# Both queries-and-keys units ahead of both v units in steps 0 and 2, and a new table of PSUM banks

## The reference

```python
def _attention(xq, xkv, wq, wk, wv, wo, bo):
    q = (xq @ wq).reshape(B, S, N_HEADS, D_HEAD)
    k = (xkv @ wk).reshape(B, T, N_HEADS, D_HEAD)
    v = (xkv @ wv).reshape(B, T, N_HEADS, D_HEAD)
    attn = jax.nn.softmax(jnp.einsum('bihd,bjhd->bhij', q, k) * D_HEAD ** (-0.5), axis=-1)
    return jnp.einsum('bhij,bjhd->bihd', attn, v).reshape(B, S, D_ATTN) @ wo + bo
h = _layernorm(x, ln1_g, ln1_b)
x = _attention(h, h, sa_wq, sa_wk, sa_wv, sa_wo, sa_bo) + x
h = _layernorm(x, ln2_g, ln2_b)
x = _attention(h, cond_emb, ca_wq, ca_wk, ca_wv, ca_wo, ca_bo) + x
h = _layernorm(x, ln3_g, ln3_b)
a, gate = jnp.split(h @ ff_w1 + ff_b1, 2, axis=-1)
return a * jax.nn.gelu(gate, approximate=False) @ ff_w2 + ff_b2 + x
```

## Time and profile before

| | us |
|---|---|
| median of 3 runs | 2865.21 |
| lowest, highest | 2864.95, 2866.52 |
| the profiled execution, device time | 2866.01 |
| its span, first to last instruction | 2864.2 |
| TensorE busy in the span | 2842.0 |
| VectorE, ScalarE, GpSimd busy | 2256.3, 1912.3, 1471.1 |

### The profile page before, as it was taken

The page is one execution under the profiler, slowest core; times in us unless marked ns, Lnnn a source line. Parts: engine busy times, 40 slices in busy tenths (PEclk is TensorE's granted clock), DMA queues, the critical chain, the costliest instruction groups (busy, mean ns, idle before and its releaser), DMA issues.

```text
span 2864.2 us, 72446 instructions
## 1 busy us (share of the span) xinstructions
PE 2842.0 (99%) x25278; PEld 2485.3 (87%) x25278; DVE 2256.3 (79%) x3495; ACT 1912.3 (67%) x6041; POOL 1471.1 (51%) x1310
## 2 busy tenths in 40 slices
PE   8999999999999999999999999999999999999999
PEld 6888888888888888888888888888888889999999
DVE  6888888888888888888888888888888865555554
ACT  6677766677766776777777777777777754444443
POOL 5444444444444444765555555555555544554554
PEclk9999999999999999999999999999999999999999
DMA  5666666666666666667777776666766632222222
GB/s 147 158 162 157 156 157 159 158 154 145 151 151 154 150 148 149 161 166 177 177 172 169 173 171 169 168 164 165 168 168 163 151 100 88 73 73 84 81 73 63
DMA packets 355360, 413.32 MB, mean 144 GB/s; under 512 B 122048, under 2 KB 209472, under 8 KB 355264
## 3 DMA queue, kind: packets, MB, share of 16 engines
q1 hardware_dynamic: 345120, 395.29, 57.4%
q10 hardware_dynamic: 10144, 16.78, 1.6%
HBM read 94.52 MB, written 49.02 MB: 50 GB/s over the span
## 4 chain that ended last, share of the span: by engine, by line
PE 98%; DVE 1%; ACT 1%; POOL 0%; issue 0%; DMA 0%; DVEq 0%; POOLq 0%; ACTq 0%
PE unit_ps L593 54%; PE o_ps L618 17%; PE s_ps L606 14%; PE s_ps L593 12%; DVE neg_max L1021 0%; ACT probs L851 0%; DVE blocks L1035 0%; POOL probs L1253 0%; DMA x_ln<-in_x_dram 0%; ACT qk_hi L882 0%; DVE qk_lo L1046 0%; DVE hT L1016 0%; DVE hT_lo L1059 0%; ACT x_n L828 0%; ACT L828 0%
## 5 line engine op out<-in xcount | busy, mean ns | idle before, releaser
L1253 POOL TENSOR_TENSOR probs<-probs,row_inv 128x1024 f32<-128x1024 f32 x512 | 967.8, 1896 | 893.9 <-DVE row_inv L1026 893.9
L851 ACT ACTIVATE probs<-s_ps,neg_max 128x256 f32<-128x256 f32 x2048 | 950.4, 487 | 403.9 <-DVE neg_max L1021 403.4
L1021 DVE TENSOR_REDUCE neg_max<-s_ps 128x4 f32<-128x1024 f32 x512 | 616.8, 1205 | 62.8 <-PE s_ps L606 58.4
L1035 DVE STREAM_TRANSPOSE blocks<-probs 128x1024 f32<-128x1024 f32 x512 | 633.2, 1237 | 19.9 <-POOL probs L1253 19.9
L593 PE MATMUL unit_ps<-hT_hi,w_hi 128*128 128x256 f32 x2048 | 571.3, 282 | 3.0 <-DVE hT_lo L1059 2.6
L593 PE MATMUL unit_ps<-hT_hi,w_lo 128*128 128x256 f32 x2048 | 554.0, 277 | 0.0
L618 PE MATMUL o_ps<-pT,v_f 128*64 128x256 f32 x4096 | 498.5, 385 | 1.7 <-DVE a_lo L1041 1.7
L593 PE MATMUL unit_ps<-hT_lo,w_hi 128*128 128x256 f32 x1792 | 496.1, 277 | 0.0
L851 ACT ACTIVATION_READ_ACCUMULATOR probs<-s_ps,neg_max 128x1 f32 x2048 | 444.6, 217 | 0.0
L593 PE MATMUL unit_ps<-w_hi,a_hi 128*128 128x256 f32 x1536 | 430.8, 280 | 3.8 <-DVE a_lo L1041 2.8
L593 PE MATMUL unit_ps<-w_lo,a_hi 128*128 128x256 f32 x1536 | 425.7, 277 | 0.0
(11 more groups left out here) (73 smaller groups left out, 6017.8 us busy)
## 6 DMA issues: line engine op xcount, KB each, us to landing
pT<-blocks SPq DMA_DIRECT2D x1024, 256.0 KB, 4.5
rows_t_dram<-row_blocks SPq DMA_DIRECT2D x91, 256.0 KB, 4.4
rows_in<-rows_t_dram SPq DMA_DIRECT2D x91, 256.0 KB, 4.1
x_res<-in_x_dram SPq DMA_DIRECT2D x32, 256.0 KB, 4.1
x_sa_dram<-x_out SPq DMA_DIRECT2D x32, 256.0 KB, 4.3
x_ln<-x_sa_dram ACTq DMA_DIRECT2D x32, 256.0 KB, 4.9
ctx_in<-in_ctx_dram SPq DMA_DIRECT2D x32, 256.0 KB, 4.4
x_res<-x_sa_dram SPq DMA_DIRECT2D x32, 256.0 KB, 4.1
```

What stands on the lines that cost most here:

```text
L851: op = nc.scalar.activation(probs[:, m % 2, r, :].rearrange("p (j b c) -> p j b c", j=IT, c=BLK), scored.rearrange("p (j c b) -> p j b c", ...
L1021: nc.vector.tensor_reduce(neg_max[:, m % RING, :], s_ps[:, m % 2, :, :].rearrange("p h (i j) -> p (h i) j", j=S), AX_X, ALU.max, negate=Tr ...
L1035: nc.vector.transpose(blocks[:, n % 2, :, m % 2, :].rearrange("p b (j r c) -> p r j b c", j=IT, c=BLK), probs[:, m % 2, :, :].rearrange("p ...
L1253: nc.gpsimd.tensor_tensor(probs[:, m % 2, :, :], probs[:, m % 2, :, :], row_inv[:, m % RING, :].unsqueeze(2).broadcast_to([P, ROWS, S]), A ...
```

## The change

In steps 0 and 2 of STEP_UNITS both qk units are put ahead of both v units; in step 2 the x unit moves behind the two qk units. BANK_OF gets a new table. The order lists of the other engines are not edited, but two of them read STEP_UNITS: evacuated_early now picks both qk units in steps 0 and 2, and bank_free finds other last users.

```diff
 STEP_UNITS = (
-    ((("v", 0, 0), "cur"), (("qk", 2), "cur"), (("qk", 3), "cur"), (("v", 0, 1), "cur")),
+    ((("qk", 2), "cur"), (("qk", 3), "cur"), (("v", 0, 0), "cur"), (("v", 0, 1), "cur")),
     ((("qk", 4), "cur"), (("qk", 5), "cur"), (("wo", 0), "prv")),
-    ((("v", 1, 0), "cur"), (("x",), "nxt"), (("qk", 6), "cur"), (("qk", 7), "cur"), (("v", 1, 1), "cur")),
+    ((("qk", 6), "cur"), (("qk", 7), "cur"), (("x",), "nxt"), (("v", 1, 0), "cur"), (("v", 1, 1), "cur")),
     ((("qk", 0), "nxt"), (("qk", 1), "nxt"), (("wo", 1), "prv")),
 )
-BANK_OF = {("v", 0, 0): 0, ("qk", 2): 2, ("qk", 3): 1, ("v", 0, 1): 0,
-           ("qk", 4): 2, ("qk", 5): 1, ("wo", 0): 0,
-           ("v", 1, 0): 2, ("x",): 0, ("qk", 6): 1, ("qk", 7): 0, ("v", 1, 1): 2,
-           ("qk", 0): 1, ("qk", 1): 0, ("wo", 1): 2}
+BANK_OF = {("qk", 2): 0, ("qk", 3): 1, ("v", 0, 0): 2, ("v", 0, 1): 0,
+           ("qk", 4): 1, ("qk", 5): 2, ("wo", 0): 0,
+           ("qk", 6): 1, ("qk", 7): 2, ("x",): 0, ("v", 1, 0): 0, ("v", 1, 1): 1,
+           ("qk", 0): 0, ("qk", 1): 1, ("wo", 1): 2}
```

## The result

| | before | after |
|---|---|---|
| median, us | 2865.86 (4 runs) | 2905.51 (4 runs) |
| lowest to highest, us | 2864.95 to 2867.11 | 2905.33 to 2907.89 |
| the profiled execution, us (span) | 2866.01 (2864.2) | 2907.89 (2906.1) |

The ratio is 1.0138, 95% interval 1.0125 to 1.0152. Slower by 1.4%, 39.7 us.

What follows compares the result with a forecast made beforehand. TensorE, busy for 2842.0 of 2864.2 us, was taken to bound the kernel. Terms 33.9 + 4.8 + 1.0 + 0.7 = +40.4 us on a median of 2865.21 gave 2905.6 us, range 2892 to 2911.

Steps and rivals of the forecast that it cites:

- The loops have no slack: Attention loops: TensorE has work every microsecond, so any wait added to it is paid in full.
- The order by itself: Steps 0 and 2, both halves: TensorE's new unit order alone saves 0.01 us a step, -1.3 us in the whole kernel.
- Cross-attention, +33.9 us: Steps 0 and 2: second v waits for VectorE's first qk_lo, 0.54 us late, net 0.53, in 64 steps.
- more than forecast: Rival: the later second v pushes its copy or the attend into the next step, delaying VectorE there; 2912 us, chance 0.05.
- Self-attention, +4.8 us: Steps 0 and 2, t = 2 to 31: second v late by 0.09 us, net 0.08, in 60 steps; range 0 to 6.
- The start, +1.7 us: At t = 1: second v late in step 0, +1.0 us, and the v behind x late in step 2, +0.7.
- The restart is free: Rival: weight loads run ahead of the wait, saving 0.11 us a step in cross-attention; 2893.0 us, chance 0.12.
- The remainder is in time: Rival: the first qk_lo ends before the second v is due, so no slowdown; 2865.6 us, chance 0.06.
- The clock: Rival: new pauses might cost TensorE its clock; low clock at the start might change by 2.8 or 1.4 us; no chance given.
- What would show it: Profile after: second v waits for qk_lo 128 times or nearly, 0.2 to 0.4 us idle each in cross-attention; TensorE busy 98%.

Runs made afterwards that it cites:

- experiment 4: Changed kernel with step 2 back in the old order, its banks making no unit wait for its own step's remainder: 2887.97 us, ratio 1.008 to before.
- experiment 1: Changed kernel with the second v of steps 0 and 2 put into a bank of s_ps: 2864.16 us, ratio 0.9995 to before.
- Experiment 3: Changed kernel with VectorE making the first qk_lo ahead of a_lo in steps 0 and 2: 2880.74 us, ratio 1.0054 to before.

## Why the prediction was right

2905.6 us was forecast and 2905.51 measured. That the two agree to 0.1 us is luck: +40.4 was forecast on a median of 2865.2, +39.7 was measured on one of 2865.9, and the two profiled executions lie 41.9 apart in span. Where TensorE starts its attends divides these 41.9: +0.4 up to t = 1, step 3 (91.46 before, 91.89 after), +4.3 to the end of self-attention, +35.2 to the last step of t = 63 (2307.71 and 2347.63), +1.9 behind it. The forecast had 1.7, 4.8, 33.9 and 0. So the mechanism and its two large terms were right, and the small ones missed by 1 or 2 us in both directions. Term by term, in the profiled executions:

- *The loops have no slack*: right. A wait in one step is not made up in another (experiment 4).
- *The order by itself, -0.01 a step*: it is -0.02 (4.99 against 5.01, experiment 1), -2.1 us over the loops instead of -1.3.
- *Cross-attention, +33.9 us*: the late start of the second v is 0.55, forecast 0.54; qk_lo ended 4.15 behind the first unit's start (1528.89 - 1524.74), forecast 4.14. Two step-0 blocks, one batch apart, in the chain in order of time of the kernel before (start, length) are 34.91 us apart:

```profile
1475.30 5.01 PE unit_ps L593 x32
...
1510.21 5.01 PE unit_ps L593 x32
```

  After, a batch takes 36.00 (in the same view its scores start at 1523.20 and those of the next batch at 1559.21), so 32 batches cost 35 us. That the next step is not pushed further (the rival *more than forecast*) shows in VectorE's first row: it waits the same 0.28 for the scores.
- *Self-attention, +4.8 us* (0 to 6): the least certain term, and right to within 1 us. Two blocks of units one batch apart, before (36.71 us) and after (36.85), in the chain in order of time:

```profile
517.15 5.70 PE unit_ps L593 x36
...
553.86 5.70 PE unit_ps L593 x36
...
519.22 5.79 PE unit_ps L593 x36
...
556.07 4.07 PE unit_ps L593 x29
```

  So 30 batches cost 4.2. In the rows below, after, the second v came 0.23 behind the first one's last matmul, so on time, but the next one 0.32 behind it: only the head start of the weight load is lost, about 0.09. The load before it stands at 504.48, so this one was due at 504.71; it comes at 504.92, right behind the end of qk_lo (504.87), and the next matmul 0.34 behind it, as at 1528.94. The view of waits doesn't show this.

```profile
504.71 0.40 PE L593 MATMUL unit_ps<-w_lo,hT_hi 128*128 128x512 f32 x1
504.94 0.48 PE L593 MATMUL unit_ps<-w_hi,hT_hi 128*128 128x512 f32 x1
505.26 0.39 PE L593 MATMUL unit_ps<-w_hi,hT_lo 128*128 128x512 f32 x1
...
504.92 0.19 PEld L593 LDWEIGHTS unit_ps<-w_hi,hT_hi 128*128 128x128 f32 x1 [0.25 <-DVE qk_lo L1046]
```

- *The start, +1.7 us*: its two waits were right, its sum was not. At t = 1, step 0, the second v came at 61.00 where 60.00 was due (59.77 + 0.23), with the restart 1.1 late as forecast, and in step 2 the v behind x started 79.77 - 78.08 = 1.69 behind x, forecast 1.67. But the start as a whole costs 0.4; the shorter stretch of low clock there (below) may be why.

```profile
78.08 0.60 PE L683 MATMUL unit_ps<-ident,x_n 128*128 128x128 f32 x4
79.77 0.50 PE L593 MATMUL unit_ps<-w_hi,hT_hi 128*128 128x512 f32 x1 [1.09 <-DVE hT L1016]
```

- *The restart is free* (the rival by the rule of the Trainium skill, "TensorE: Matmul & The Clock Gate", Step-by-step, on weight loads pulled ahead of matmuls in flight): wrong here. The load at 1528.94 started with its matmul, so here the load was not pulled ahead of the wait. Had it been free, a step would have lost 0.44 instead of 0.55.
- *The remainder is in time*: wrong, with a_lo ahead of it. Experiment 3 shows that a_lo decides: it gives back 25 us of the 40 by that one exchange.
- *The clock*: no pause in the loops touched it (1.00 in both stretches). At the two ends it moved. At the start and at the drain after:

```profile
34.00:39.20 5.20, 5.20 (x44) 4.98 (x41) 4.69 (x5) 3.68 (x11) 2.27 (x2) 0.67 0.45 139
2349.00:2363.00 14.00, 11.19 (x71) 9.41 (x68) 10.84 (x12) 7.94 (x7) 7.59 (x3) 0.76 0.70 184
```

  and at the drain before:

```profile
2309.00:2313.00 4.00, 1.24 (x11) 0.59 (x6) 3.15 (x5) 3.31 (x3) 3.12 (x2) 0.93 0.89 221
2313.00:2319.00 6.00, 5.95 (x40) 5.22 (x40) 6.00 (x6) 3.32 (x3) 0.38 (x1) 0.76 0.93 250
```

  A share of 0.67 over 5.20 us means 3.4 us at half clock, where before it was all of 5.70; at the drain 0.76 over 14.00 means 6.7 us, where before it was 3.4. I had no such term in the sum. As far as TensorE was at work in these stretches, half of their length is time lost: by this estimate up to 1.1 us less at the start and up to 1.7 more at the drain. That is the size of the two misses there (0.4 instead of 1.7, and 1.9 instead of 0), but no run takes the low clock out of the changed kernel, so this is argued and not shown. Executions of the changed kernel lie up to 2.6 us apart (the profiled one is the longest), and these stretches of low clock are of that size; that they make up that spread I only infer.
- *What would show it*: the waits were to be 128, with TensorE at 98%. The view counts 65, one of them at t = 1, as the short ones of self-attention leave no idle time to be counted, and the page says 99% (2866.0 of 2906.1 is 98.6).

## What to carry to other kernels

Where banks rotate and the engine that writes them has no slack, the price of a table is read off in one subtraction: when the last reader of a bank ends, by its own engine's list, against when the next writer is due. Of two readers, the one that stands late in a list without gaps on another engine makes the bank late in every turn of the loop; moving that one reader up, or giving the writer another bank, was worth far more here (25 and 41 us, experiments 3 and 1) than the order of the writers (2 us). And the loss is not the idle time that the profile shows: here 18.4 us of waits stood for some 40 us, since the matmul before is shown as busy into each pause (0.40 from its start, the next one due at 0.23) and the restart hides in the busy time. Count distances from start to start.

## What the hardware showed beyond that

A wait of TensorE cost 0.11 us more than its length (at 1528.94 the next start at 0.34 instead of 0.23), and 0.09 even where it was over 0.02 before the matmul was due (504.92; the next start at 0.32 instead of 0.23): in these rows the release had to come ahead of the weight load, which otherwise starts 0.22 ahead of its matmul (1528.05 and 1528.27), not of the matmul. The granted clock fell to 0.50 behind a stretch of 3.50 us with 0.34 us of work, and it did not when the stretch was filled (3.12 us of work).
